# Broader blocks of targets in a dense graph attention layer: 13 or 12 windows to a step in place of 7 or 6

## The reference, cut to what matters

```python
h = einsum('nf,hfu->nhu', atom_features, W)
scores = leaky_relu(alpha_src[src] + alpha_dst[dst], 0.2)
att = exp(clip(scores, -2.0, 2.0))
att_norm = att / segment_sum(att, src)[src]
out = segment_sum(h[dst] * att_norm, src)
return leaky_relu(out.reshape(N, -1) @ merge_kernel, 0.2)
```

## Time and profile before

| engine | busy us | share of the span |
|---|---|---|
| TensorE, matmul | 3125.2 | 60% |
| VectorE | 3109.6 | 60% |
| ScalarE | 1812.4 | 35% |
| GpSimd | 1698.0 | 33% |

### The profile page before, as it was taken

The page is one execution under the profiler, slowest core; times in us unless marked ns, Lnnn a source line. Parts: engine busy times, 40 slices in busy tenths (PEclk is TensorE's granted clock), DMA queues, the critical chain, the costliest instruction groups (busy, mean ns, idle before and its releaser), DMA issues. The chain is left out here.

```text
span 5205.2 us, 45137 instructions
## 1 busy us (share of the span) xinstructions
PE 3125.2 (60%) x11765; PEld 2024.9 (39%) x11765; DVE 3109.6 (60%) x4761; ACT 1812.4 (35%) x2737; POOL 1698.0 (33%) x1687
## 2 busy tenths in 40 slices
...
GB/s 31 99 90 101 197 214 213 152 124 115 119 122 120 122 119 96 181 181 183 63 49 52 99 51 51 50 35 30 27 39 34 39 33 32 38 33 29 6 52 28
DMA packets 294100, 448.72 MB, mean 86 GB/s; under 512 B 180002, under 2 KB 183965, under 8 KB 284439
## 3 DMA queue, kind: packets, MB, share of 16 engines
...
...
## 5 line engine op out<-in xcount | busy, mean ns | idle before, releaser
L896 PE MATMUL l_sum_ps<-arena,sums 125*65 125x500 f32 (+1 forms) x2600 | 1155.7, 584 | 248.1 <-DVE arena L790 218.7
L1814 POOL DMA_INDIRECT l_rows<-table,tile_src x782 | 770.1, 985 | 351.8 <-issue 222.4
L1225 POOL DMA_INDIRECT l_rows<-hidden_rows,tile_src x782 | 787.5, 1007 | 238.1 <-issue 238.1
L779 DVE SCALAR_TENSOR_TENSOR arena<-arena,far_past 125x750 f32<-125x750 f32 (+1 forms) x800 | 805.3, 1046 | 17.8 <-DMA arena<-score_rows 17.8
L825 ACT ACTIVATE arena<-arena,far_left 125x750 f32<-125x750 f32 (+1 forms) x800 | 716.9, 950 | 166.9 <-DVE arena L779 166.8
L1278 PE MATMUL l_acc_ps<-l_rows,l_hot 128*125 x1612 | 360.9, 413 | 649.2 <-DVE l_rows L1242 635.5
L790 DVE SCALAR_TENSOR_TENSOR arena<-arena,l_turned 125x1500 f32<-125x1500 f32 (+1 forms) x400 | 710.7, 1777 | 49.3 <-ACT arena L830 42.8
L896 PEld LDWEIGHTS l_sum_ps<-arena,sums 125*65 125x65 f32 x2600 | 334.6, 139 | 1003.9 <-issue 544.3
L830 ACT ACTIVATE arena<-arena 125x1500 f32<-125x1500 f32 (+1 forms) x400 | 601.4, 1504 | 0.0
L1278 PEld LDWEIGHTS l_acc_ps<-l_rows,l_hot 128*125 128x125 f32 x1612 | 340.1, 321 | 671.0 <-issue 668.7
L1242 DVE TENSOR_TENSOR l_rows<-l_rows,l_attr 128x512 f32<-128x512 f32 x98 | 68.4, 698 | 814.8 <-DMA l_rows<-hidden_rows,tile_src 814.8
...
## 6 DMA issues: line engine op xcount, KB each, us to landing
...
```

The lines of the kernel that those rows point to most:

```text
L779: last = v.scalar_tensor_tensor(scores(k)[:, i, :], rows[:, 1, i, :], m.far_past[:, w, h:h + 1], rows[:, 0, i, :], ALU.add, ALU.max)
L896: last = nc.tensor.matmul(sum_ps[0:F + 1, c, 0:hi - lo], h_one[:, w, :], z[k % ZS][:, lo:hi], start=(w == 0), stop=(w == W - 1))
L1225: pool.indirect_dma_start(rows[:, b % RING, t, :], None, m.hidden_rows[:, :], bass.IndirectOffsetOnAxis(ap=m.tile_src[:, k:k + 1], axis=0) ...
L1814: pool.indirect_dma_start(rows[:, t % RING3, :], None, m.table3[:, :], bass.IndirectOffsetOnAxis(ap=m.tile_src[:, t:t + 1], axis=0)).then_ ...
```

## The change

- From the second quarter on a pair of heads has two blocks, of 13 and 12 windows, in place of four. The stage has 4 + 6 = 10 blocks, and 100 + 150 = 250 steps. `add`, `bend`, `rise` and `weigh` keep their number of instructions per step. The first quarter keeps its blocks.
- Three tiles of the new width (`BROAD_ZS`) lie over the old ring of six; the transposed counts have five wide buffers (`BROAD_TURNS`), of which two lie over the raw buffers. For this the raw buffers of the first quarter go from six to four.
- From the second quarter on VectorE's order is `weigh(k)`, `add(k + 2)`, and ScalarE's `bend(k)`, `rise(k)`.
- The sums take seven PSUM banks (26 or 24 cells), so `heads` has one bank. It and `divide` and `gather` go by pieces of one head and at most 7 windows, after steps 2, 5, 8, 11 (`heads`) and 4, 7, 10, 13 (`divide`) of the next block. There are 3 whole pieces (the first three blocks), 2 of the fourth block and 24 of the six broad ones. `gather` is one GpSimd instruction per piece.
- `evict` comes between `bend` and `rise` of the next block's step 1, and takes two or three instructions where it took one or two; it waits for all `heads` of the block before.

```diff
 SCORED, JOINED, SETTLED = 4, 7, 10
+BROAD_BLOCKS = [(0, 13), (13, 12)]
+BROADEST, BROAD_ZS, BROAD_TURNS = 13, 3, 5
+IN_SUMS = 12
-RAWS = 6
+RAWS = 4
...
-    blocks = [(p, w0, n) for p in range(0, H, PAIR) for w0, n in BLOCKS]
+    blocks = [(0, w0, n) for w0, n in BLOCKS] + [(p, w0, n) for p in range(PAIR, H, PAIR) for w0, n in BROAD_BLOCKS]
+    narrow = len(BLOCKS)
+
+    pieces = [(b, None, 0, blocks[b][2]) for b in range(narrow - 1)]
+    for b in range(narrow - 1, len(blocks)):
+        for i in range(PAIR):
+            pieces += [(b, i, lo, min(WIDEST, blocks[b][2] - lo)) for lo in range(0, blocks[b][2], WIDEST)]
+    pieces_of = [[q for q in range(len(pieces)) if pieces[q][0] == b] for b in range(len(blocks))]
     steps = [(b, w) for b in range(len(blocks)) for w in range(W)]
...
-        share = m.arena[0:P, used:used + PAIR * WIDEST * F].rearrange("p (h w f) -> p h w f", h=PAIR, f=F)
+        broad = PAIR * BROADEST * P
+        more = s.sb("more", [P, broad + PAIR * WIDEST * F])
+        share = more[:, broad:].rearrange("p (h w f) -> p h w f", h=PAIR, f=F)
+        broad_near = [[near[0], more[:, 0:broad]], [near[1], m.arena[0:P, used:used + broad]]]
+        assert used + broad <= m.arena.shape[1]
+        at_z, at_raw = m.arena[0:P, 0:ZS * PAIR * size], m.arena[0:P, (ZS * PAIR + 4 * PAIR) * size:(ZS * PAIR + 4 * PAIR + RAWS) * size]
+        broad_z = [at_z[:, i * PAIR * size:i * PAIR * size + broad] for i in (4, 0, 2)]
...
-        count_ps, sum_ps = s.ps("count_ps", (128, 2, 512)), s.ps("sum_ps", (128, 4, 512))
-        head_ps = s.ps("head_ps", (128, PAIR, 512))
+        at_turned = turned[:, :, :].rearrange("p a n -> p (a n)")
+        broad_turned = [at_raw[:, 0:2 * size], at_turned[:, 4 * size:6 * size], at_raw[:, 2 * size:4 * size],
+                        at_turned[:, 0:2 * size], at_turned[:, 2 * size:4 * size]]
+        sum_ps = s.ps("sum_ps", (128, 8, 512))
+        count_ps, head_ps = sum_ps[:, 0:2, :], sum_ps[:, 6:8, :]
...
         def scores(k):
-            return z[k % ZS][:, 0:PAIR * count(k) * P].rearrange("p (h n) -> p h n", h=PAIR)
+            here = z[k % ZS] if k < FIRST else broad_z[(k - FIRST) % BROAD_ZS]
+            return here[:, 0:PAIR * count(k) * P].rearrange("p (h n) -> p h n", h=PAIR)
+        def scores_free(k):
+
+            if k < FIRST:
+                return k - ZS + 1
+            return (FIRST - 4, FIRST - 2, FIRST)[k - FIRST] if k < FIRST + BROAD_ZS else k - BROAD_ZS + 1
         def turned_counts(k):
-            return turned[:, k % TURNS, 0:count(k) * P]
+            here = turned[:, k % TURNS, :] if k < FIRST else broad_turned[(k - FIRST) % BROAD_TURNS]
+            return here[:, 0:count(k) * P]
...
-        def near_rows(b):
-            return near[b % 2][:, 0:2 * PAIR * blocks[b][2] * P].rearrange("p (a h n) -> p a h n", a=2, h=PAIR)
+            return turned_in[(k - FIRST) % BROAD_TURNS], 32 * ((k - FIRST) // BROAD_TURNS + 1)
+
+        def near_rows(b, a):
+            if b < narrow:
+                here = near[b % 2][:, a * PAIR * blocks[b][2] * P:]
+            else:
+                here = broad_near[b % 2][a]
+            return here[:, 0:PAIR * blocks[b][2] * P].rearrange("p (h n) -> p h n", h=PAIR)
+
+        def summed_cell(b, i, w):
+            cell = i * blocks[b][2] + w
+            if b < narrow:
+                return sums[b % 2][:, cell * P:(cell + 1) * P]
+            return sums[0][:, cell * P:(cell + 1) * P] if cell < IN_SUMS else sums[1][:, (cell - IN_SUMS) * P:(cell - IN_SUMS + 1) * P]
...
             def load_turned(k):
                 b, w = steps[k]
                 _, w0, n = blocks[b]
-                sp.wait_ge(weighed, k - TURNS + 1)
-                if k - TURNS < FIRST:
-                    sp.wait_ge(*stored(k - TURNS))
-                if k < 2 * FIRST:
-                    sp.wait_ge(*stored(k - FIRST))
+                if k == FIRST:
+                    sp.wait_ge(count_ready, FIRST - 2)
+                elif k == FIRST + 1:
+                    sp.wait_ge(weighed, FIRST - 4)
+                    sp.wait_ge(*stored(FIRST - 6))
+                    sp.wait_ge(*stored(FIRST - 5))
+                elif k == FIRST + 2:
+                    sp.wait_ge(count_ready, FIRST)
+                elif k < FIRST + BROAD_TURNS:
+                    sp.wait_ge(weighed, FIRST - 2 if k == FIRST + 3 else FIRST)
+                    sp.wait_ge(*stored(FIRST - 4 if k == FIRST + 3 else FIRST - 2))
+                    sp.wait_ge(*stored(FIRST - 3 if k == FIRST + 3 else FIRST - 1))
+                else:
+                    sp.wait_ge(weighed, k - BROAD_TURNS + 1)
+                if b < narrow + len(BROAD_BLOCKS):
+                    for c, (first, wide) in enumerate(BLOCKS):
+                        if w0 <= first < w0 + n:
+                            sp.wait_ge(*stored(W * c + w))
                 for lo, hi in ((0, WIDE), (WIDE, P)):
                     sp.dma_start(turned_counts(k)[lo:hi, :], m.turned_counts[w, lo:hi, w0 * P:(w0 + n) * P]
-                                 ).then_inc(turned_in[k % TURNS], 16)
+                                 ).then_inc(turned_in[(k - FIRST) % BROAD_TURNS], 16)
...
-            def gather(b):
-                p, w0, n = blocks[b]
-                here = m.gathered[:, w0:w0 + n, :]
-                pool.wait_ge(shared, b + 1)
-                if p == 0:
+            def gather(q):
+                b, i, lo, n = pieces[q]
+                p, w0, _ = blocks[b]
+                here = m.gathered[:, w0 + lo:w0 + lo + n, :]
+                pool.wait_ge(shared, q + 1)
+                if i is None:
                     g.tensor_tensor(here, share[:, 0, 0:n, :], share[:, 1, 0:n, :], ALU.add).then_inc(gathered, 1)
-                    return
-                g.tensor_tensor(here, here, share[:, 0, 0:n, :], ALU.add).then_inc(kept, 1)
-                pool.wait_ge(kept, b - len(BLOCKS) + 1)
-                g.tensor_tensor(here, here, share[:, 1, 0:n, :], ALU.add).then_inc(gathered, 1)
-            for b in range(len(blocks)):
-                gather(b)
+                elif p == 0 and i == 0:
+                    g.tensor_copy(here, share[:, q % 2, 0:n, :]).then_inc(gathered, 1)
+                else:
+                    pool.wait_ge(gathered, q)
+                    g.tensor_tensor(here, here, share[:, q % 2, 0:n, :], ALU.add).then_inc(gathered, 1)
+            for q in range(len(pieces)):
+                gather(q)
...
                 if w == 0:
                     dve.wait_ge(near_in[b % 2], 32 * (b // 2 + 1))
                 if k >= ZS:
-                    dve.wait_ge(summed, k - ZS + 1)
-                rows = near_rows(b)
+                    dve.wait_ge(summed, scores_free(k))
...
-            def divide(b):
-                n = blocks[b][2]
-                got = head_ps[0:P, :, 0:n * (F + 1)].rearrange("p h (w f) -> p h w f", f=F + 1)
...
+            def divide(q):
+                b, i, lo, n = pieces[q]
+                if i is None:
+                    got = head_ps[0:P, :, 0:n * (F + 1)].rearrange("p h (w f) -> p h w f", f=F + 1)
+                    left, to = inv[:, :, 0:n], share[:, :, 0:n, :]
+                else:
+                    got = head_ps[0:P, 1:2, 0:n * (F + 1)].rearrange("p h (w f) -> p h w f", f=F + 1)
+                    left, to = inv[:, 0:1, 0:n], share[:, q % 2:q % 2 + 1, 0:n, :]
+                dve.wait_ge(heads_ready, q + 1)
+                v.tensor_scalar(left, got[:, :, :, F], 1e-30, None, ALU.max).then_inc(inv_ready, 1)
+                dve.wait_ge(inv_ready, 2 * q + 1)
+                v.reciprocal(left, left).then_inc(inv_ready, 1)
+                dve.wait_ge(inv_ready, 2 * q + 2)
+                if q:
+                    dve.wait_ge(gathered, q if i is None else max(narrow - 1, q - 1))
+                v.tensor_tensor(to, got[:, :, :, 0:F], over(left.unsqueeze(3), (P, 2 if i is None else 1, n, F)), ALU.mult).then_inc(shared, 1)
...
             for k, (b, w) in enumerate(steps):
                 weigh(k)
-                if k + 3 < len(steps):
+                if k + 3 < FIRST:
                     add(k + 3)
-                if b and w == 4:
-                    divide(b - 1)
-            divide(len(blocks) - 1)
+                elif FIRST <= k + 2 < len(steps):
+                    add(k + 2)
+                if b and w >= 4 and (w - 4) % 3 == 0 and (w - 4) // 3 < len(pieces_of[b - 1]):
+                    divide(pieces_of[b - 1][(w - 4) // 3])
+            for q in pieces_of[-1]:
+                divide(q)
...
             def evict(b):
-                n = PAIR * blocks[b][2]
+                n, first = PAIR * blocks[b][2], 2 if b < narrow else 0
                 act.wait_ge(summed, W * (b + 1))
                 if b >= 2:
...
+                    act.wait_ge(heads_ready, pieces_of[b - 2 if b < narrow else b - 1][-1] + 1)
+                parts = [(0, n, sums[b % 2])] if b < narrow else [(0, IN_SUMS, sums[0]), (IN_SUMS, n, sums[1])]
```

(46 more changed lines are left out.)

25 lines of the change are left out of this document (4 added, 21 removed).

## The result

| | median us (runs) | range | ratio, 95% interval |
|---|---|---|---|
| before | 5209.3 (6) | 5205.5 to 5213.8 | 1 |
| after | 5187.4 (6) | 5180.5 to 5199.5 | 0.9961 (0.9948 to 0.9973) |

The change makes the kernel 20 us faster by the ratio, 22 by the medians; the forecast was 44, to 5163, in a range of 5150 to 5188. So the sign was right and the size was not: half the gain is missing, and the median lies at the very edge of the range. The profiled execution of after has a span of 5185.2 us and a time of 5187.0.

A forecast was written before the change was run, and what follows sets the result against it. VectorE, busy 97.97 of 100 us from the second quarter on, was taken as the bound. Terms -48.8 + 4.5 - 0.8 - 13.6 + 5 + 9.6 gave -44 us, so 5163 us, range 5150 to 5188.

The forecast's parts named there:

- 1. Fewer VectorE instructions: VectorE's steps from the second quarter on: 150 broad steps replace 300 narrow ones, saving fixed instruction cost, -48.8 us.
- rival A: VectorE's merged instructions: each saves only 0.065 us, not add's 0.13, so -29 us and a time of 5183; 6%.
- 2. The other engines: Broad steps: ScalarE, TensorE and the tile ring keep up with VectorE's 7.10 us, cost 0.
- 3. Transfers: Loads of counts and score rows, including the handover: all arrive in time, cost 0, bounds 0 and +5 us.
- Rival C: Loads behind load_near come 7 us late, five times, and the gain is gone: 5198 us; 5%.
- 4. Divide: VectorE's divides, now by pieces of one head and at most 7 windows: 20.9 us for 16.4, +4.5 us.
- 5. Gather: VectorE's adds stretched while GpSimd adds: same elements in as many instructions, -0.8 us, bounds -3 and +3.
- 6. Block ends: VectorE's stalls behind ScalarE at block ends: 24.4 us go, 10.8 come, -13.6 us.
- Rival D: Block ends cost nothing, the clock does not matter and gather hides in weigh: 5148 to 5155 us; 5%.
- 7. TensorE over the block's end: TensorE idles during evict, its clock falls, and VectorE's add waits about 1 us six times: +5 us, bounds 0 and +15.
- rival B: TensorE's low clock stays in broad steps, making them 11 us; at 20 such steps 5243 us; 5%.
- 8. The end: After the last weigh: the last pieces run one after the other, 21.9 us for 13.2, +9.6 us with its stall.

The follow-up runs named there:

- raws6: The changed kernel, masked, with six raw buffers in place of four: 5213.3 us, 1.0004 of the unmasked kernel before.
- raws4: The kernel before, masked, with four raw buffers in place of six: 5224.8 us, 1.0032 of the unmasked kernel before.
- evict_early: The changed kernel, masked, with score rows split into four transfers and a broad block's first sums awaiting only the eviction's first part: 5472.2 us, 0.9931 of unmasked before.
- masked kernels: Experiment kernels with two register values of the counting stage masked to 16 bits: attention stage 1541.4 to 1545.4 us as before, 1515.9 to 1519.3 as after.

## Why the prediction was half right

**1. Fewer VectorE instructions: right.** 7.10 us a step of 13 windows, 6.58 of 12, as worked out; the fixed cost of `add` goes with the instruction, so rival A is out. **2. The other engines: right.** ScalarE 6.1 us, TensorE 5.67 and 5.25; no wait of VectorE outside the block ends but one of 0.36.

**3. Transfers: this step failed.** "Behind a `load_near` of 3.25 MB it waits 15 us at 214 GB/s", cost 0, was worked out for the broad part, where the load behind it has 28 us of lead, and it held there. But the first of these loads is issued in the fourth narrow block, where the raw counts behind it have 14 us by the prediction's own working, and SyncE's issues come up 12 us late. At the 189 and 193 GB/s of 850 to 870 us the 3.25 MB alone are 17 us, an estimate, while the quarter's own traffic takes 205 to 214 all the time. Bandwidth alone doesn't explain it, since the DMA engines' mean busy share falls to 0.34 in it. The step looked at the first quarter only for the raw buffers, which raws6 and raws4 show to be harmless. The cost was put at 0, at most 5; the two stalls are 13.2 us, and splitting gave 14.1 back. The prediction's own test, a first quarter more than 5 us longer, shows it: 11.4. Rival C had the mechanism and the wrong place: no load was late in the broad part.

**4. Divide: right.** 0.88 us for 6 cells and 0.97 for 7, against 0.93 and 1.00. **5. Gather: too small.** The count was right, 22 lengthened `add`s in place of 23, but they are 0.63 us longer each and not 0.78 as before (4.08 for a pair of 3.46), 13.9 us in all for 18.0. That is -4.1 for a forecast of -0.8, just outside its bound of -3.

**6. Block ends: right.** 11.8 us in seven stalls, longest 1.9, for 10.8 in six; the two at the handover are 1.9 and 0.9 for 1.1 together. Rival D is out.

**7. TensorE over the block's end: right mechanism, too small.** Seven waits of 10.3 us in place of 5, inside its bound of 15. At the handover the granted clock of 975 to 980 is 0.50, which is 1.2 GHz, and VectorE's `add` at 983.44 waits 2.1 us. evict_early takes nearly all of it away: 9 to 11 us of the stage were in the wait for the whole eviction and the lower clock behind it. Over the broad part the granted clock is 0.97, so rival B is out. The Trainium skill, Perfetto Trace Analysis, section Optimizing Tensor Performance, which the prediction named here, wants a group's copying out to run beside the next group's matmuls. evict_early does that with the first banks of a block, and its trace agrees: 10.1 us of waits become 1.3.

**8. The end: right.** Stall 2.6 for 2.4; from the last `weigh`'s end at 2045.93 to the last gather's at 2069.00 23.1 us for 21.9.

With 13.2 for term 3, 5.3 more for term 7, 1.4 for term 8, 1.0 for term 6, 3.3 less for term 5 and 0.9 less for term 4, the sum of -44 becomes -27. The masked kernels measured -26 in the stage, the unmasked pair, one execution each, -31; that difference is open.

**Not in the prediction at all**: the 11 us given back behind the stage by instructions that the diff does not touch. 782 + 782 gathers of 6 to 7 ns more are 10 of the 13.5 us by which their stages grow. The prediction read no row of those stages. So what it missed is term 3, by 13 us, and the stages behind, which its sum took as unchanged without a reason, by 11 us. The misses of the other terms partly cancel, which is luck.
